# The sum of the edge attributes reads a PSUM bank that ScalarE fills in quarters

## The reference

```python
h_low  = relu(segment_sum(w_low[:, None]  * (x @ W_low)[src],  dst))    # layer 0
h_high = relu(segment_sum(w_high[:, None] * (x @ W_high)[src], dst))
...
row = edge_index[0]                                                      # layer 1: by source node
seg_sum = segment_sum(edge_attr, row)                                    # 32 attributes an edge
seg_max = segment_max(edge_attr, row)
cnt     = segment_sum(ones, row)
seg_mean = seg_sum / maximum(cnt, 1.0)
h = concatenate([seg_sum, where(cnt > 0, seg_max, 0), seg_mean, u[batch]])
```

## Time and profile before

| | before |
|---|---|
| median of 3 runs | 9233.94 us |
| lowest and highest | 9219.14, 9248.25 us |
| span of the profiled execution | 9369.1 us |
| the profiled execution's own time | only its span is given |
| TensorE busy | 5537.1 us (59%) |
| VectorE busy | 5345.0 us (57%) |
| GpSimd busy | 4789.4 us (51%) |
| ScalarE busy | 1663.2 us (18%) |
| mean granted TensorE clock | 0.731 |
| first pass (51 blocks), `place` to `place` | about 62 us a block |

### The profile page before, as it was taken

One profiled execution on the slowest core, in us unless ns is written; L12 is line 12 of the kernel. 1 busy time (PEld: TensorE's weight loads), 2 busy tenths in 40 slices (PEclk: granted clock), 3 DMA queues, 4 the chain that ended last, 5 costly groups with the idle time before them and its releaser, 6 DMA issues. The chain is left out here.

```text
span 9369.1 us, 138875 instructions
## 1 busy us (share of the span) xinstructions
PE 5537.1 (59%) x49076; PEld 4542.6 (48%) x49077; DVE 5345.0 (57%) x9166; ACT 1663.2 (18%) x3235; POOL 4789.4 (51%) x4394
## 2 busy tenths in 40 slices
PE   2555555555555523233455542899996677777777
PEld 1333333333333322223345441899995566666665
DVE  5555655565556533334344455666665677777773
ACT  0111111111111100002111131000002333333333
POOL 3555555555555454550355551455550577667670
PEclk7666676666666666665666675999996788888885
DMA  3222222221222154441100030111110333333330
GB/s 98 77 82 78 73 75 81 78 78 70 81 78 80 40 92 89 88 88 29 42 20 19 20 109 12 26 26 27 27 27 17 106 100 97 95 93 95 95 92 13
DMA packets 392774, 612.74 MB, mean 65 GB/s; under 512 B 158383, under 2 KB 318995, under 8 KB 377363
## 3 DMA queue, kind: packets, MB, share of 16 engines
q1 hardware_dynamic: 240826, 478.03, 16.7%
q0 software_dynamic: 141056, 124.52, 6.4%
q10 hardware_dynamic: 10454, 4.04, 0.2%
HBM read 531.52 MB, written 216.25 MB: 80 GB/s over the span
## 5 line engine op out<-in xcount | busy, mean ns | idle before, releaser
L321 POOL DMA_INDIRECT pay_d<-row,place x1632 | 1719.7, 1054 | 1524.9 <-DVE place L497 947.9
L415 PE MATMUL win<-onehot,val 128*128 128x128 f32 x4998 | 1045.4, 353 | 672.4 <-issue 455.3
L415 PEld LDWEIGHTS win<-onehot,val 128*128 128x128 f32 x4998 | 872.3, 251 | 926.8 <-issue 644.4
L514 DVE TENSOR_TENSOR onehot<-near_dve,drel 128x896 f32<-128x896 f32 x357 | 389.3, 1091 | 1182.2 <-remote 1057.4
L2113 POOL DMA_INDIRECT m_from_src<-from_src_d,m_row x510 | 684.0, 1341 | 628.5 <-issue 375.4
L1712 PE MATMUL g_win<-g_hot,y_part 128*128 128x128 bf16 x14994 | 880.7, 220 | 145.1 <-DVE g_hot L1761 101.1
L1692 POOL DMA_INDIRECT g_x<-xg_d,g_row x510 | 641.5, 1258 | 625.1 <-PE g_win L1712 411.7
L1712 PEld LDWEIGHTS g_win<-g_hot,y_part 128*128 128x128 bf16 x14994 | 857.3, 99 | 166.8 <-DVE g_hot L1761 102.1
L1091 POOL DMA_INDIRECT sorted_d<-s_row,s_place x510 | 494.1, 969 | 531.0 <-DVE s_place L1207 368.5
L672 POOL DMA_INDIRECT r_x<-in_x,r_row x510 | 485.2, 951 | 500.9 <-DMA r_row<-pay_d 351.2
L2116 POOL DMA_INDIRECT m_from_dst<-from_dst_d,m_row x510 | 631.0, 1237 | 160.0 <-issue 155.7
(11 more groups left out here) (410 smaller groups left out, 11491.4 us busy)
## 6 DMA issues: line engine op xcount, KB each, us to landing
m_hot_t<-drow_d SPq DMA_DIRECT2D x52, 1568.0 KB
scan_d<-in_none SPq DMA_DIRECT2D x51, 1034.2 KB
lo_row<-lo_d SPq DMA_DIRECT2D x51, 1024.0 KB
m_grid<-pay_d SPq DMA_DIRECT2D x52, 882.0 KB
pay_d<-in_fill SPq DMA_DIRECT2D x51, 882.0 KB
grid<-pay_d SPq DMA_DIRECT2D x51, 882.0 KB, 3.8
pay_d<-in_fill SPq DMA_DIRECT2D x51, 720.0 KB
row<-in_pay SPq DMA_DIRECT2D x51, 576.0 KB
```

The source lines that it names most:

```text
L321: pool.indirect_dma_start(a["pay_d"][:, :], bass.IndirectOffsetOnAxis(ap=place[j][:, c:c + 1], axis=0), row[j][:, c, :], None).then_inc(ro ...
L415: mm(win[:, :], val[u % 2][:, s, :], onehot[u % 2][:, s, :], start=(u == 0 and s == 0), stop=(u == NS - 1 and s == SUB - 1))
```

## The change

`close_grid` held three VectorE instructions on the whole grid: the sum (`total`), `tmp` (attributes plus a penalty for empty cells), and the maximum (`most`). After the change `tmp` comes first and in one piece. Sum and maximum are cut into quarters of 12, 12, 12 and 13 slots and alternate. The sum no longer reads the grid in SBUF but a PSUM bank, `attr`, into which ScalarE copies one quarter at a time: quarter 0 ahead of the last `hot` of the block, quarters 1 to 3 after it, each after VectorE's sum has read the quarter before. To make room for the bank, `tot` moves into the unused end of a bank of `pair`. The grid's buffer is given back after the last quarter, where it was given back after `tmp`.

```diff
-        tot = ps("tot", [P, 512])[:, 0:2 * CB]
+        tot = pair[1][:, 1, BK * NT:BK * NT + 2 * CB]
+        attr = ps("attr", [P, 512])
+        attr_ready, attr_used = sem("attr_ready"), sem("attr_used")
+        NQ = 4
+        quarters = [slice(q * NT // NQ, (q + 1) * NT // NQ) for q in range(NQ)]
...
+                def attrs(b, i, j, q):
+                    part = quarters[q]
+                    wait(act, attr_used, b * NQ + q)
+                    sc.activation(attr[:, 0:(part.stop - part.start) * F].rearrange("p (s f) -> p s f", f=F), grid[j][:, part, 0:F],
+                                  ACT.Copy).then_inc(attr_ready, 1)
+
                 def mark(b, i, j):
                     for u in range(NS):
+                        if u == NS - 1:
+                            act.wait_ge(grid_in[j], i * 16 + 16)
+                            attrs(b, i, j, 0)
                         act.wait_ge(val_ready, b * NS + (u + 1))
                         sc.activation(hot16[u % 2][:, :], onehot[u % 2][:, :, :].rearrange("p s w -> p (s w)"),
                                       ACT.Copy).then_inc(hot16_ready, 1)
+                    for q in range(1, NQ):
+                        attrs(b, i, j, q)
...
                 def close_grid(b, i, j):
                     base = dve.value_load(k.base_i[0:1, at(b)], min_val=0, max_val=z.n)
-                    v.tensor_tensor(k.total[:, :].rearrange("p (s f) -> p s f", f=F), grid[j][:, :, 0:F],
-                                    k.total[:, :].rearrange("p (s f) -> p s f", f=F), ALU.add)
                     v.tensor_tensor(tmp[:, :, :], grid[j][:, :, 0:F], pen.unsqueeze(2).to_broadcast([P, NT, F]), ALU.add)
-                    dve.drain().then_inc(grid_used, 1)
-                    v.tensor_tensor(k.most[:, :], k.most[:, :], tmp[:, :, :].rearrange("p s f -> p (s f)"), ALU.max)
+                    for q, part in enumerate(quarters):
+                        flat = slice(part.start * F, part.stop * F)
+                        dve.wait_ge(attr_ready, b * NQ + (q + 1))
+                        v.tensor_tensor(k.total[:, flat], attr[:, 0:flat.stop - flat.start], k.total[:, flat], ALU.add).then_inc(attr_used, 1)
+                        if q == 0:
+                            dve.drain()
+                        v.tensor_tensor(k.most[:, flat], k.most[:, flat], tmp[:, part, :].rearrange("p s f -> p (s f)"), ALU.max)
+                    dve.sem_inc(grid_used, 1)
                     dve.wait_ge(sub_done, b * NS + NS)
```

## The result

The changed kernel takes 9546.12 us (median of 5 runs, 9531.42 to 9576.85) beside 9233.94 us of the kernel before (5 runs, 9218.95 to 9248.25): ratio 1.0339, 95% interval 1.0322 to 1.0355. It is 312 us slower, where I forecast 66 us faster. The profiled execution took 9550.74 us with a span of 9549.1, so this profile stands for its runs better than that of before did, whose span lay 135 us above its median.

What follows compares the result with a forecast made beforehand. A first-pass loop through GpSimd's scatters and VectorE bounds the kernel. Per block 2.04 - 0.5 - 0.16 = 1.38 us, over 49 blocks 67.6 less 1.8 at the end, 65.8: 9234 - 66 = 9168, range 9121 to 9209 (0.74).

Steps and rivals of the forecast that it cites:

- the loop has nothing else that changes: First pass, `place` to `place`: only scatter time changes, 1.38 us a block less.
- 0.82 + scatters + 3.3 + 15.0: First-pass block: `place` to first scatter, the scatters, last scatter to VectorE's resume, resume to next `place`; sum 62.13 us.
- the rule: First pass: VectorE resumes at scatter end plus 3.3 us, read from the rows.
- Two of the signs that I had named: First pass: resume still 3.3 to 3.4 us after the last scatter; GpSimd's idle before `place` still 19.3 us a block.
- The removal of the hold: Scatters beside `close_grid`: 2.04 us hold lost, less 0.5 for maxima and 0.16 for `lo_hot`, gives 1.38 us a block.
- of the maxima one catches: `close_grid`: four maxima with two SBUF operands catch one scatter, 0.5 us a block; bounds none (0), two (1.1).
- VectorE's order in `close_grid`: Quarters timed from `tmp`: maximum 3 starts at 5.70, L532 at 6.21; `close_grid` grows by 0.89 us.
- The cover of 22 us: VectorE's idle before the resume hides `close_grid`'s growth of 0.89 us; without it 44 us.
- the rival within 0.3%: Maxima and `lo_hot` catch what the sum let go, or `deg` becomes last: 9209 to 9234; chance 0.15.
- The rival on the other side: SP's transfers, from `lo_hot`, set VectorE's resume, so 0.89 us is paid each block: +44, 9278; chance 0.10.

Runs made afterwards that it cites:

- e15_after_third: The changed kernel, unaltered, beside the kernel before on the chip with 7633.39 us: 7616.56 us, 0.9986.
- e14_paced_after_again: The changed kernel with three GpSimd pauses (memset and drain) ahead of the 9th, 17th and 25th scatter: 8881.11 us, 0.9473 against the kernel before.
- e2_late_vector: The kernel before plus one VectorE instruction in `close_grid` (grid plus pen, one operand in PSUM): 9372.73 us, 1.0002.
- e13_after_again: The changed kernel, unaltered, measured again beside the kernel before on a chip with 9385.71 us: 9673.24 us, 1.0308.
- e1_free_scatters: The kernel before, `total` and `most` replaced by same-size instructions with one PSUM operand: 9651.99 us against 9374.38, 1.0308.
- e18_quarters_third: The changed kernel, the sum's quarters reading the grid in SBUF, without `attr` bank and ScalarE's copies: 9374.39 us against 9236.62 for the kernel before, 1.0146.
- e16_quarters_again: The changed kernel, the sum's quarters reading the grid in SBUF, without `attr` bank and ScalarE's copies: 7654.19 us against 7633.39 for the kernel before, 1.0024.
- e3_pause_early: The changed kernel with four GpSimd memsets, each with a drain, ahead of the 9th scatter: 9672.68 us against 9374.38 for the kernel before, 1.0318.

## Why the prediction was wrong

**The step that failed** is one sentence of the sum: "the loop has nothing else that changes". It took the loop as 0.82 + scatters + 3.3 + 15.0, with 3.3 a constant and VectorE's 22 us of idle as slack, and so counted a faster scatter as pure gain. Measured in the block above, the scatters gave 1.6 us and the resume went from 3.41 to 11.09 us after them. The constant was no constant but the sign of a wait: signals come late while scatters run, and in the kernel before only the last handoffs of a block fell into that time. I had the row that says so. TensorE's matmul done at 1562.43, VectorE released at 1567.84, 5.4 us later, and I wrote that "the trace doesn't say why its signal counts only after the scatters", then took the rule on without asking which other handoffs it would catch. Two of the signs that I had named show it: the resume was to stay 3.3 to 3.4 us after the last scatter, and GpSimd's idle time before `place` at 19.3 us; it rose to 26.1 (1306.0 over 50).

**The removal of the hold** was right in kind, and too small: 1.38 us a block forecast, 1.92 measured (94.1 us over 49). `total` no longer holds GpSimd, and of the maxima one catches for 0.32 us where I took 0.5.

The Trainium skill (SBUF — State Buffer, section Who interferes with whom) says that a VectorE instruction with at most one SBUF input, outside the modes that use two ports, doesn't contend with GpSimd. This case's trace agrees: the scatters beside `tmp` and the first sums out of the bank take 0.97 us. Whether such freedom is a gain is another matter; in these runs it came with a loss of 3%.

**VectorE's order in `close_grid`** was right to 0.1 us up to the last maximum (5.60 after `tmp`, forecast 5.70). Then 0.84 us of "issue" stand ahead of L551 that weren't there before, so 7.02 in place of 6.21. That gap isn't the kernel's own: the same kernel on the chip with 7633.39 us (`e15_after_third`) starts L551 6.09 us after `tmp` (1042.73 less 1036.64), with no idle time, and so does `e14_paced_after_again` in most blocks. The groups by line put 41.2 of the changed kernel's 49.8 us of idle time there down to "remote", so it looks like another signal that comes late. It costs little either way: `e2_late_vector`, later by as much, ran at 1.0002.

**The cover of 22 us** was there, but not for everything. VectorE may be late (`e2_late_vector`); TensorE's counts may not, since they have to pass ahead of the spell. I named `deg` as a possible last wait, in the rival within 0.3%, and not the counts of the next block, 7.1 us of TensorE's and ScalarE's work that moves behind the scatters as a whole.

**The rival on the other side** (VectorE's wait ended by a fixed time from `lo_hot`, 9278) didn't happen either. The side it named was right by chance; the resume still hangs on the end of the scatters.

**The step from 264 to 312 us.** The two traces differ by 263.7 us in the first pass, the medians by 312, the spans by 180. The kernel before's profiled execution had 135 us more than its median, and I can't say in which stage. By these two traces the pass carries 264 of the 312. There is a better pair: `e13_after_again`, the changed kernel on a chip where the kernel before takes 9385.71 us, starts its scatters from 98.6 to 3538.4 us, 291 us more than the trace of before, against a loss of 287.5 between the medians. The trace of before, with its span of 9369.1, looks like one from such a chip, which the record doesn't say; if it is, the first pass carries the whole loss.

What stays open: what in the chip makes the signals late; what exactly begins a spell (20 us or some 15 scatters without a break of about 1 us fit the blocks of the kernel before, the changed one and `e1_free_scatters`, but not the second block of `e18_quarters_third`, and no run varied the two apart); and why it is there on the chips that take 9234 to 9386 us for the kernel before, and not on those that take 7633 and 7642.

## What to carry to other kernels

A wait that ends when another engine's work ends, though the program doesn't tie the two, isn't a constant to build on: list the handoffs that lie close ahead of it, and ask which of them fall in when that other work gets denser. A stall that seems pure loss can be the gap through which signals pass; before removing one, try its opposite, a pause put in by hand, which here was worth 4 to 5% (0.9588, 0.9503, 0.9473). And measure such a tuning on more than one chip: the same pauses cost 5% (1.0516) where signals weren't late.

## What the runs showed of the hardware

In a spell, on the chips where it occurs, it isn't signals alone that are late: SP's own steps are slow. The line that loads `row` holds a register move and the issue of a transfer. In the changed kernel, single instructions (ns min/median/max):

```profile
L306 SPq DMA_DIRECT2D row<-in_pay x51: 4/697/716, 66.8 to 3359.9; - x51
...
L306 SPq MOVE row<-in_pay x48: 4/692/1385, 150.3 to 3359.2; - x48
```

and in `e16_quarters_again`, where no signal is late:

```profile
L306 SPq DMA_DIRECT2D row<-in_pay x51: 332/333/378, 66.1 to 2241.1; - x51
...
L306 SPq MOVE row<-in_pay x48: 29/29/38, 141.5 to 2241.1; - x48
```

A move of 29 ns takes 692, an issue of 333 takes 697 (medians). In the kernel before, SP's issue of `lo_row` still took 0.33 us, 18.9 us after the first scatter, and its issue of the grid, after the last one, 0.70. Two of TensorE's matmuls in that kernel's spell:

```profile
1560.53 0.59 PE L418 MATMUL deg<-hot,ones 128*1 128x512 bf16 x1 [1.03 <-issue]
1561.95 0.48 PE L419 MATMUL deg<-hot,ones 128*1 128x384 bf16 x1 [0.84 <-issue]
```

The two start 1.42 us apart, where outside it the same pair starts 0.22 apart. It looks as if an engine's instruction queue advanced by one instruction each 0.70 us, a weight load and a matmul being two of them. That is my reading and isn't shown: in `e3_pause_early` the same pair starts 2.32 us apart, and in the changed kernel's spell eight matmuls of the counts took 1.68 us (1528.20), as long as outside it.

The chips differ by more than any kernel here: 7642.20 and 7633.39 us on two, 9233.94 to 9385.71 on the others, for one and the same program, the mean granted TensorE clock 0.80 and 0.73 beside them. And a drain of GpSimd among its scatters costs 2 us, the first in a block 2 to 7 (3.3 us, and 3.6 to 8.5, from start to start against 1.27).
